# Attention stage of a graph network: the products of the shifts behind the source products, and the row multiplication at the head of the next tick

## The reference

```python
lin_x = x @ W_lin.T + b_lin
feat = concat([x[src], edge_weights, x[dst]], axis=1)       # 64 + 16 + 64
h = relu(feat @ W_att1.T + b_att1)
scores = (h @ W_att2.T + b_att2)[:, 0]
m = segment_max(scores, src)
e = exp(scores - m[src])
denom = segment_sum(e, src)
msg = segment_sum((e / denom[src])[:, None] * lin_x[dst], src)
```

## Time and profile before

| what | value |
|---|---|
| median of 3 runs | 7888.26 us (7883.47 to 7888.82) |
| profiled execution, span | 7885.51 us, 7883.6 us |
| busy over the span | PE 4875.0, DVE 4538.2, ACT 2058.9, POOL 5047.4 us |
| instructions of L899 (one a tick) | 468 |

### The profile page before, as it was taken

One profiled execution on the slowest core, in us unless ns is written; L12 is line 12 of the kernel. 1 busy time (PEld: TensorE's weight loads), 2 busy tenths in 40 slices (PEclk: granted clock), 3 DMA queues, 4 the chain that ended last, 5 costly groups with the idle time before them and its releaser, 6 DMA issues.

```text
span 7883.6 us, 169485 instructions
## 1 busy us (share of the span) xinstructions
PE 4875.0 (62%) x30913; PEld 3631.3 (46%) x30914; DVE 4538.2 (58%) x19982; ACT 2058.9 (26%) x5709; POOL 5047.4 (64%) x9951
## 2 busy tenths in 40 slices
PE   6333666566533475555555555555568888888887
PEld 3333333333333454444434444444446666666665
DVE  5666677677532482332323233232369999999997
ACT  4000000000000052222222222222235555555555
POOL 1666666666666446666666666666668878878886
PEclk9555555555555586667676666676689999999999
DMA  7222222222222224323222222222243443443443
GB/s 257 46 49 50 46 48 48 48 48 48 48 51 50 41 71 126 96 92 95 92 90 89 89 91 90 89 90 91 89 125 102 103 102 101 103 102 101 102 103 97
DMA packets 1160316, 670.13 MB, mean 85 GB/s; under 512 B 797187, under 2 KB 1060948, under 8 KB 1159396
## 3 DMA queue, kind: packets, MB, share of 16 engines
q1 hardware_dynamic: 1020628, 422.54, 21.8%
q0 software_dynamic: 137728, 243.98, 10.7%
q10 hardware_dynamic: 1888, 2.83, 0.1%
HBM read 371.08 MB, written 311.42 MB: 87 GB/s over the span
## 4 chain that ended last, share of the span: by engine, by line
another core or an unknown queue 15%; issue 15%; POOL 11%; PE 6%; DMA 4%; DVE 4%; ACT 3%; SPq 2%; DVEq 1%; POOLq 1%; ACTq 0%
PE banks L1402 4%; DMA wide<-rows_by_src 3%; POOL ring L875 2%; SPq L723 2%; ACT ring L1091 1%; ACT ring L1098 1%; POOL rows_by_src L841 1%; POOL ring L899 1%; DVE wide L2011 1%; POOL ring L893 1%; DVE wide L2016 1%; POOL ring L885 1%; DMA rows_by_src<-ring 1%; POOL ring L869 1%
## 5 line engine op out<-in xcount | busy, mean ns | idle before, releaser
L841 POOL DMA_INDIRECT rows_by_src<-ring x1760 | 1704.4, 968 | 1055.8 <-issue 517.8
L813 POOL DMA_INDIRECT wide<-msg_table,ring x1664 | 1576.5, 947 | 1062.8 <-issue 558.9
L1402 PE MATMUL banks<-wide,ring 128*128 x3520 | 1348.1, 513 | 938.1 <-ACT ring L1091 650.3
L1402 PEld LDWEIGHTS banks<-wide,ring 128*128 128x128 f32 x3520 | 793.7, 278 | 1192.2 <-issue 1150.2
L1316 PE MATMUL banks<-wide,ring 128*128 x3520 | 860.1, 426 | 680.0 <-DVE ring L1814 339.0
L1316 PEld LDWEIGHTS banks<-wide,ring 128*128 128x128 f32 x3520 | 784.9, 328 | 759.2 <-issue 758.7
L1098 ACT COPY ring<-banks 128x416 f32<-128x416 f32 x880 | 405.8, 518 | 1855.9 <-remote 1217.3
L1974 DVE COPY ring<-ring 128x4 f32<-128x4 f32 x440 | 81.8, 186 | 1353.0 <-DMA rows_by_src<-ring 1092.4
L1779 DVE TENSOR_TENSOR acc<-acc,banks 128x64 f32 x1760 | 389.2, 221 | 787.9 <-issue 269.1
L1443 PE MATMUL banks<-wide,ring 128*128 x5616 | 741.9, 282 | 2.2 <-ACT ring L1135 2.1
L1443 PEld LDWEIGHTS banks<-wide,ring 128*128 128x128 bf16 x5616 | 492.7, 98 | 160.5 <-issue 4.1
(11 more groups left out here) (334 smaller groups left out, 9797.6 us busy)
## 6 DMA issues: line engine op xcount, KB each, us to landing
wide<-rows_by_src SPq DMA_DIRECT2D x1872, 105.0 KB, 2.0
ring<-attr_turned SPq DMA_DIRECT2D x440, 128.0 KB
attr_turned<-ring SPq DMA_DIRECT2D x416, 96.0 KB
rows_by_src<-ring POOLq DMA_INDIRECT x1760
wide<-msg_table,ring POOLq DMA_INDIRECT x1664
ring<-attr_by_dst SPq DMA_DIRECT2D x208, 64.0 KB
attr_turned<-ring SPq DMA_DIRECT2D x208, 64.0 KB
attr_by_dst<-in_edge_attr_dram SPq DMA_DIRECT2D x1, 13281.2 KB
```

What stands on the lines that cost most here:

```text
L813: g.indirect_dma_start(out=A_g[:, b * GV + u, :], out_offset=None, in_=table[:, :], in_offset=bass.IndirectOffsetOnAxis(ap=A_idx[:, b * GV ...
L841: g.indirect_dma_start(out=rows_d[:, :], out_offset=bass.IndirectOffsetOnAxis(ap=B_pos[:, s, u:u + 1], axis=0), in_=B_row[:, s, u, :], in_ ...
L1402: mm(b, B_DT[:, t, u, :], qh[:, w, :].rearrange("p a k -> p (a k)"), start=True, stop=False)
```

## The change

Four engines get another order in a tick; the instructions stay the same.

- PE: L1423 stands behind L1443 and in front of L1451, with one more wait, for the scan of stage 3 of this tick (the scan's input `C_tm` lies in the same PSUM bank as the result of L1423).
- DVE: L2029 stands behind the two L2016.
- ACT: L1123 becomes stage 5 and is first in the tick; L1132 stands in front of L1128.
- POOL: L899 becomes stage 5. The tick begins with the wait for stage 2's score (`c_s`), then L899, L859, L868 to L870, L885 to L894, and L875 and L877 last.

```diff
 # POOL
             def tick(i, s, stages):
+                if 2 in stages:
+                    after_c(pool, c_s, *stages[2], incs=2)
+                if 5 in stages:
+                    t, j = stages[5]
+                    after_c(pool, c_p, t, j)
+                    after_c(pool, c_ag, t, j, 2)
+                    g.tensor_tensor(C_W[:, t % 2, :, :], C_V[:, t, :, H1:ROW_SRC],
+                                    per_group(C_p[:, t, :], HID + 1), ALU.mult).then_inc(c_W, 1)
                 if 0 in stages:
...
                 if 2 in stages:
...
-                    after_c(pool, c_s, t, j, incs=2)
...
-                if 4 in stages:
-                    t, j = stages[4]
-                    after_c(pool, c_mg, t, j)
-                    after_c(pool, c_p, t, j, CS)
-                    ch.link(g.tensor_tensor(C_z[:, t, :], C_s[:, t, :], C_mg[:, t, :], ALU.subtract))
-                    turn(pool, "pool")
-                    g.tensor_scalar(C_d[:, t, :], C_z[:, t, :], 0.0, None, ALU.min).then_inc(c_d, 1)
                 if 3 in stages:
...
                 if 4 in stages:
                     t, j = stages[4]
-                    after_c(pool, c_p, t, j)
-                    after_c(pool, c_ag, t, j, 2)
-                    g.tensor_tensor(C_W[:, t % 2, :, :], C_V[:, t, :, H1:ROW_SRC],
-                                    per_group(C_p[:, t, :], HID + 1), ALU.mult).then_inc(c_W, 1)
+                    after_c(pool, c_mg, t, j)
+                    after_c(pool, c_p, t, j, CS)
+                    ch.link(g.tensor_tensor(C_z[:, t, :], C_s[:, t, :], C_mg[:, t, :], ALU.subtract))
+                    turn(pool, "pool")
+                    g.tensor_scalar(C_d[:, t, :], C_z[:, t, :], 0.0, None, ALU.min).then_inc(c_d, 1)
 # ACT
             def tick(i, s, stages):
+                if 5 in stages:
+                    t, j = stages[5]
+                    after_c(act, c_d, t, j)
+                    after_c(act, c_W, t, j, CS)
+                    a.activation(C_p[:, t, :], C_d[:, t, :], ACT.Exp).then_inc(c_p, 1)
                 if 2 in stages:
...
-                    after_c(act, c_d, t, j)
-                    after_c(act, c_W, t, j, CS)
-                    a.activation(C_p[:, t, :], C_d[:, t, :], ACT.Exp).then_inc(c_p, 1)
...
 # PE: the block of stage 4 from the head of the tick to behind stage 1, with
+                    if 3 in stages:
+                        after_c(pe, c_new, *stages[3])
...
 # DVE: the block of stage 4 from the head of the tick to behind the two add_parts
```

More of the change, by code:

```diff
@@ L896, in tick @@
                     t, j = stages[4]
-                    after_c(pool, c_p, t, j)
-                    after_c(pool, c_ag, t, j, 2)
-                    g.tensor_tensor(C_W[:, t % 2, :, :], C_V[:, t, :, H1:ROW_SRC],
-                                    per_group(C_p[:, t, :], HID + 1), ALU.mult).then_inc(c_W, 1)
-            run_ticks(pool, tick, 5, ch, CS * (2 + 1 + 4), CS, C_LOOPS)
+                    after_c(pool, c_mg, t, j)
[3 more added lines that the diff above has]
+                    g.tensor_scalar(C_d[:, t, :], C_z[:, t, :], 0.0, None, ALU.min).then_inc(c_d, 1)
+            run_ticks(pool, tick, 6, ch, CS * (2 + 1 + 4), CS, C_LOOPS)
             def with_features(k):
@@ L1120, in tick @@
                     a.activation(C_cr[:, t, :], C_df[:, t, :], ACT.Exp).then_inc(c_cr, 1)
-                    after_c(act, c_d, t, j)
-                    after_c(act, c_W, t, j, CS)
-                    a.activation(C_p[:, t, :], C_d[:, t, :], ACT.Exp).then_inc(c_p, 1)
+                if 0 in stages:
+                    after_c(act, c_N, s, i)
+                    after_c(act, c_ag, s, i, CS)
+                    a.activation(C_S[:, s, :, :], C_N[:, s, :, :], ACT.Identity, bias=ones[:, 0:1], scale=-1.0).then_inc(c_S, 1)
                 if 2 in stages:
@@ L1129, in tick @@
                 if 0 in stages:
-                    after_c(act, c_N, s, i)
-                    after_c(act, c_ag, s, i, CS)
-                    a.activation(C_S[:, s, :, :], C_N[:, s, :, :], ACT.Identity, bias=ones[:, 0:1], scale=-1.0).then_inc(c_S, 1)
                     after_c(act, c_St, s, i)
@@ L1135, in tick @@
                     a.activation(C_STb[:, s, :, :], four(bank_b[0], P), ACT.Identity, bias=ones[:, 0:1], scale=-1.0).then_inc(c_STc, 1)
-            run_ticks(act, tick, 5, None, 0, CS, C_LOOPS)
+            run_ticks(act, tick, 6, None, 0, CS, C_LOOPS)
             act.wait_ge(n_ones, 1)
@@ L1417, in tick @@
                     r = regs(ENG.PE, wpair_of, j1 * (C_BODY // 2) + t1 * PV, N_WIN - 1, PV)
[L1418 to L1424, removed]
                 if 3 in stages:
@@ L1445, in tick @@
                             last.then_inc(c_pre, 1)
+                if 4 in stages:
+                    t, j = stages[4]
+                    after_c(pe, c_mn, t, j)
+                    after_c(pe, c_mg, t, j, 1)
+                    if 3 in stages:
+                        after_c(pe, c_new, *stages[3])
+                    for u in range(GV):
+                        last = mm(bank[5][:, u * PARTS:(u + 1) * PARTS], C_STb[:, t, u, :], C_mp[:, t, u // 2, :], start=True, stop=True)
+                    last.then_inc(c_mm, 1)
                 if 2 in stages:
@@ L2024, in tick @@
                     m_acc = ch.do(add_sums(0))
[L2025 to L2029, removed]
                 if 3 in stages:
@@ L2057, in tick @@
                     add_parts(1)
+                if 4 in stages:
+                    t4, j4 = stages[4]
+                    after_c(dve, c_mm, t4, j4)
+                    after_c(dve, c_d, t4, j4, CS)
+                    v.tensor_reduce(C_mg[:, t4, :], bank[5][:, 0:GV * PARTS].rearrange("p (u k) -> p u k", k=PARTS), AX.X, ALU.add).then_inc(c_mg, 1)
+                if 1 in stages:
                     dve.wait_ge(c_add, (j1 * CS + t1) * 2 + 1)
```

## The result

The changed kernel takes 8089.44 us (median of 4 runs, 8087.0 to 8095.39), the kernel before on the same chip 7887.37: ratio 1.0258, 95% interval 1.024 to 1.0276. The forecast was 8057 us, within 7915 to 8150. The change makes the kernel slower, in the way forecast, by 202 us where 170 were expected.

A forecast was written before the change was run, and what follows sets the result against it. A ring of waits through L1423 bounded the kernel, GpSimd being fullest. New tick 3.31 + 0.45 + 0.82 = 4.58 us, 0.36 more; times 468 ticks, 168 us on 7885.5, plus 2.7 to the median: 8057 us, range 7915 to 8150.

The forecast's parts named there:

- The ring of one GpSimd tick plus three ScalarE instructions: GpSimd's whole tick, then L1123, L1114, L1115 before its next: 4.58 us a tick, 0.36 more than before; chance 0.75.
- The link: From GpSimd's last instruction L877 through ScalarE's L1123, L1114, L1115 to GpSimd's next L899: 0.82 us, bounds 0.70 and 1.00.
- The collision with the comparison: VectorE's comparison L2049 holds up GpSimd's split at L869 or L870 each tick: 0.45 us, bounds 0.2 and 0.7.
- GpSimd's run without collisions: GpSimd's own instructions and gaps in one tick, start to start, when nothing holds them up: 3.31 us.
- the wait before the shift products: TensorE's wait at L1423 for GpSimd's L894, 0.30 us a tick, goes; nearly 1 us comes before L1451.
- no score of 0.72 us: On VectorE, scores no longer meet L899, giving back up to 0.42 us in such ticks; taken as 0.
- The loads: Row loads land 3.76 us after L899 and are wanted one tick later; the 4.58 us tick covers them.
- First rival: Faster: only the ring through L1423 mattered and the new ring is under 4.22 us; at best 7829 us; chance 0.08.
- the ring through L1423: Waits through TensorE's L1423 and mask products, VectorE's maximum and scan, GpSimd's L885 to L894; tick 4.22 us before.
- Second rival: Gain and loss cancel: ring 4.19 to 4.25 us a tick, 7870 to 7901 us; chance 0.05.
- Third rival: The path through VectorE's L2049 and the scores closes the ring: 4.33 us a tick, 7937 us; chance 0.10.
- Fourth rival: Longer TensorE waits bring its clock down to 1.2 GHz: at worst +1370 us, 9255 us as a bound; chance 0.02.

The follow-up runs named there:

- the moved wait: Changed kernel with GpSimd's wait for the score moved back from the head of the tick to the split: ratio 0.9992 to the kernel before.
- the dose: Changed kernel with ScalarE's exponential made twice, then four times, the extra results unread: ratios 1.0274 and 1.0377 to the kernel before.
- TensorE's part alone: Kernel before with only the change's TensorE and VectorE orders, GpSimd and ScalarE as before: ratio 1.0396.
- GpSimd's and ScalarE's part alone: Kernel before with only the change's GpSimd and ScalarE orders, TensorE and VectorE as before: ratio 1.0209.
- the two kernels with the late sum: Kernel before with the change's TensorE and VectorE orders, without and with L1123 moved to the end of ScalarE's tick: ratios 1.0396 and 1.019.
- the fastest: Changed kernel with the score wait back at the split and GpSimd's subtractions ahead of the shift block's last two instructions: 7836.44 us, ratio 0.9945.

## Why the prediction was right, point by point

- The ring of one GpSimd tick plus three ScalarE instructions: right, and shown by the moved wait, by the dose, and by L901 ending behind the scores in 312 of 322 ticks.
- The link: 0.82 us forecast, 0.83 measured.
- The collision with the comparison: 0.45 forecast. L876 and L877 take 592 and 255 ns against 0.20 us free: 0.39 + 0.06 = 0.45. In the tick shown L876 took 0.71 us, as L885 did in the earlier trace rows.
- GpSimd's run without collisions: 3.31 us forecast, 3.83 - 0.45 = 3.38 measured. This is the mis-sized term: 0.07 of the 0.08 us by which the tick was too short; 0.08 x 468 = 37 us, where the forecast missed the measured time by 32. The subtractions now lie beside the scores: L899 takes 265 ns where the earlier trace rows has 0.20, and 0.47 us pass from L899 to L901 in the mean instead of 0.40. That is the size of the miss, and the other differences nearly cancel. The shift's block took 1.04 us in the mean, less than its 1.10, which I had read in a tick where it already ran beside scores. The copy L870 takes 0.13 us more in every sixth tick, which the sum had left out.
- TensorE: the wait before the shift products went, 0.90 us came before the transposition ("nearly 1 us"). The extra wait for the scan, taken as 0 with 0.1 as its bound, costs 17.2 us in 40 ticks by the list of waits, 0.05 us a tick on an engine with room.
- VectorE: no score of 0.72 us is left (the longest of all 1872 took 0.34), and the tick is longer all the same, as said.
- The loads: covered, as said.
- First rival (the ring through L1423 was the bound): it falls. TensorE's part alone makes the kernel slower, and the wait that it names goes with GpSimd's new order alone. The Trainium skill's advice that I set beside this rival ("Perfetto Trace Analysis", section "Optimization Strategies") did not pick out the wait that counts: with the wait for L894 gone, GpSimd's and ScalarE's part alone is 2% slower, and TensorE's and VectorE's part alone 4% slower, the latter with a later sum that the same edit brings.
- What bounds the kernel before: my reading of the ring through L1423 was too simple, and GpSimd was not the fullest engine. VectorE is busy 372.07 of 400 us in the earlier trace rows, 3.93 us a tick, and its waits from 5900 to 7400 us are these two and one of 0.2 us:

```profile
DVE banks L2033 <- PE banks L1433: 47.5, 177, 0.3
...
DVE ring L2029 <- PE banks L1423: 20.5, 59, 0.4
```

  They make 0.19 us a tick, so by the measure that gave GpSimd 3.85 us VectorE has 4.03 of the 4.22. Part of that is time in which L899 held the scores up. Which engine or ring set the 4.22 us was not tested.
- Second rival (gain and loss cancel): it falls, at 202 us.
- Third rival: its path exists and shows in ticks of 4.50 us when the link is shortened on ScalarE's side only; in the changed kernel the scores end ahead of L901.
- Fourth rival, TensorE's clock: half seen. The granted clock was 0.97 in the stage, not 1.00, as the window that answers to the earlier trace rows has it:

```profile
6500.00:6900.00 400.00, 311.23 (x3171) 252.84 (x3170) 323.25 (x1387) 200.53 (x601) 289.44 (x1128) 0.97 0.36 92
```

TensorE waits 0.90 us a tick before one transposition there, so slower matmuls have room beside that wait. The trace bounds their cost: from 5950 to 7450 us the clock is at its lower level (1.2 GHz) in 25 short stretches, and the 50 ticks that overlap one take 4.76 us in the mean, the other 271 take 4.65. That is at most 0.02 us a tick, or 9 us of the 202. With the exponential made four times it is 4.83 us in 143 such ticks and 4.87 in the others, so no cost shows there. In the two kernels with the late sum such ticks are longer, by 0.08 and 0.10 us spread over all ticks; whether the clock or the long tick came first there is not shown.

## What to carry to other kernels

Before an instruction is put at the head of an engine's loop, follow what its wait needs round the loop: if the last instruction of the turn before feeds it through another engine, the engine's own run and that engine's latency add up and nothing covers them. A wait belongs in front of the instruction that reads the data, not earlier: here one wait moved down past the row multiplication and the keys turned the ratio of 1.0258 into 0.9992. And an engine that is busy 62% of the whole span, as GpSimd is in the changed kernel (5048.9 of 8087.3 us), can still lie on the ring that sets a stage's tick. The measure is its tick less its waits for other engines and loads, and it has to be taken for every engine.

## What the runs showed of the hardware that was not expected

TensorE's granted clock differs between these kernels, which do the same matmuls. The kernel with the exponential made four times, whose tick is 4.85 us, had 0.91 in the same 400 us:

```profile
6500.00:6900.00 400.00, 317.38 (x3042) 255.14 (x3042) 312.06 (x1331) 210.50 (x823) 277.11 (x1090) 0.91 0.36 89
```

and the fastest, with 4.11 us, had 1.00:

```profile
6500.00:6900.00 400.00, 342.93 (x3614) 280.51 (x3614) 361.39 (x1577) 219.63 (x684) 323.20 (x1284) 1.00 0.43 105
```

In these 400 us the kernels with ticks of 4.11 to 4.40 us had 1.00 and those with ticks of 4.55 to 4.87 us 0.91 to 0.98, though not in the order of the ticks: TensorE's and VectorE's part alone, at 4.87 us, had 0.97. What in TensorE's work brings it down is not shown.

The Trainium skill's page "TensorE: Matmul & The Clock Gate", section "HAM oscillation — how this bites in real kernels", says that waits between bursts of matmuls can bring the lower clock back; that the 0.97 and the 0.91 come with the longer ticks agrees with it. The cost is far smaller than my bound of 9255 us.

The second surprise is the price of an instruction on ScalarE in a chain. One more exponential, 0.19 us long, lengthened the link by 0.025 us. In the changed kernel the first score instruction starts 0.18 us behind the exponential in the mean; with one more between them it starts 0.21 us behind the first, so most of the extra one fits into a time that passed anyway. What fills that time is not shown. Each of the next two cost (1.034 - 0.854) / 2 = 0.09 us, and they start 0.095 us behind one another.
